# Multiplying the repeated u by B for two groups in one VectorE instruction

## The chip, the cores and the metric

The kernel runs on one core of a Trainium2 chip. The metric is the device time of one execution in microseconds. The kernel before took 5985.74 us (median of 3 runs, 5984.24 to 5988.39).

## What is computed

The input x is (4, 128, 64, 64) in float32. Layer 0 is a four-head attention over the 4096 positions of each image with a residual and a layer norm. Layer 1, which the change touches, is the sum of a 3x3 convolution, a spectral filter (a 1x1 mix between an rfft2 and an irfft2) and a Mamba block over the 4096 positions. The part that counts here is the selective scan of the Mamba block, for 256 channels with 16 states each:

```python
def step(h, inp):
    xt, dtt, Bt, Ct = inp
    dA = jnp.exp(dtt[..., None] * A)
    h = dA * h + dtt[..., None] * Bt[:, None, :] * xt[..., None]
    y = jnp.einsum('bdn,bn->bd', h, Ct)
    return (h, y)
```

The product dt * x is called u in the kernel. For each channel it is needed 16 times, once per state, each time multiplied by another row of B.

## The kernel before

Layer 0 runs first and writes its result to memory; layer 1 (`layer1`, from L685) starts when it has ended. The 4 images of 4096 positions are cut into 32 items of 512 positions (`NIT`), and the 256 channels x 16 states of an item into G = 32 groups of 128 rows (8 channels x 16 states). Below, g is the number of a group within its item.

Each engine has its own program, written out in order: for each item a loop over g, in which `emit` issues the work on this item and `prepare(it + 1, ...)` a slice of the preparation of the next one. Engines wait for each other with semaphores alone. For one group the work is this:

- TensorE, `repeat_u` (L1021): a 0/1 matmul copies u of 8 channels to 128 rows, in PSUM bank g % 4 (`NU = 4`). It waits until the scan of group g - 4, which read that bank, has ended (L1020).
- VectorE, `times_b` (L1181): multiplies that bank in place by `b_rep`, the rows of B. It waits for the matmul (semaphore `u_rep`).
- ScalarE, `decay` (L1119): exp(dt * A) in `d_a`, on data that SyncE's DMA queue has brought (L885).
- VectorE, the scan (L1195), which writes `hh`; then ScalarE keeps its last column (L1112).
- GpSimd, L1232: multiplies `hh` by C into `hc`.
- TensorE, `sum_states` (L1004): every four groups, it sums 16 states to one channel. It is issued in the slots g = 8, 12, ..., 28, and for the last eight groups in slots 0 and 4 of the next item. The one of slot g reads `hc` of groups g - 8 to g - 5.

VectorE multiplies one group ahead: multiply 0, multiply 1, scan 0, multiply 2, scan 1, and so on. After the scans of g = 5 and g = 21 it adds the skip term (`add_skip`, L1166), which reads the bank that `sum_states` of slots 8 and 24 begins anew (L1002 makes it wait). After the scan of g = 16 it adds one row to the output (L1172), and after the scans of g = 23 and 24 it makes the low part of the next item's u (`low`, L1154).

TensorE works strictly in the order of its program. Between the `repeat_u` of g and of g + 1 stands the other work of slot g, one or two steps in most slots: `sum_states`, a matmul of `prepare`, convolution matmuls by the table `FILLS`. Slot 29 is the longest, with 8 small matmuls in fp32 (L973, L974), and slot 30 has 4 more (L994). After the scan of g = 18 GpSimd also computes dt (L1220), after 19 ux (L1223), and after 22 `gate` (L1215).

The two lines of TensorE that the wait for a bank rests on:

```python
ge(pe, scanned, it * G + g - NU + 1)
nc.tensor.matmul(ps[:, U_BANK + g % NU, :], sel_g[:, j, :], s_u[:, p, s, :], start=True, stop=True).then_inc(u_rep, 1)
```

Of the kernel before, what the change touches and what calls it, by code (L numbers as in the profile page):

```python
# [8 lines left out]
ALU = mybir.AluOpType  # L9
# [667 lines left out]
LC = 512  # L677
# [7 lines left out]
def layer1(nc, z_ext, w, out, nb=B):  # L685
# [16 lines left out]
    with ExitStack() as ctx:  # L702
        def sb(name, shape, dt=F32):
            return ctx.enter_context(nc.sbuf_tensor(name, shape, dt))
# [8 lines left out]
        ps = ctx.enter_context(nc.psum_tensor("ps1", [128, 8, CH], F32))  # L713
        U_BANK, Y_BANK, O_BANK, ITEM_BANK = 0, 4, 5, 6
        NU = 4
# [26 lines left out]
        b_rep = sb("b_rep", [128, 2, LC])  # L742
# [19 lines left out]
        with nc.Block() as block:  # L762
            @block.sync
            def _(sp):
                for dst, src in (
                        (win[:, :], w["win"]), (xs[:, :, :, :].rearrange("p a b c -> p (a b c)")[:, 0:4 * INNER],
                                                w["taps"].rearrange("(o k) e -> o (k e)", o=1).to_broadcast([C, 4 * INNER])),
                        (wxd[:, :, :], w["wxd"]), (wdt[:, :], w["wdt"]), (sel_b[:, :], w["sel_b"]), (sel_c[:, :], w["sel_c"]),
                        (hh[:, 0:2, :].rearrange("p a b -> p (a b)"), w["sel_g"]), (sel_y[:, :, :], w["sel_y"]),
                        (wconv[:, :, :], w["wconv"]), (wspec[:, :, :], w["wspec"]), (hilb[:, :], w["hilb"]),  # L770
                        (hil0[:, :], w["hil0"].to_broadcast([128, W])), (wout[:, :, :], w["wout"]), (cols[:, :], w["cols"]),
                        (a_neg[:, :], w["a_log"])):
                    sp.dma_start(dst, src).then_inc(loaded, 16)
                sp.wait_ge(loaded, NLOAD)
# [49 lines left out]
        G = GROUPS  # L824

        def ge(e, s, value):

            if value > 0:
                e.wait_ge(s, value)  # L829

        def column(g):


            half, jj, i = g // 16, g // 4 % 4, g % 4
            return 2 * half + i // 2, jj + 4 * (i % 2)
# [6 lines left out]
        def steps(prepare, emit, tail):  # L842

            for g in range(G):
                prepare(0, 0, g)
            for it in range(NIT):
                emit(it, it % 2)
            tail()

        with nc.Block() as block:  # L850
# [297 lines left out]
            @block.vector  # L1148
            def _(dve):
                def low(j, p, stack, src, part):  # L1150

                    a, b = slice(64 * part, 64 * part + 64), slice(64 - 64 * part, 128 - 64 * part)
                    dve.wait_ge(hi_ready, j * 2 + part + 1)
                    nc.vector.tensor_tensor(stack[b, p, part::2, :], src[a, :, :], stack[a, p, part::2, :].bitcast(F32), ALU.subtract  # L1154
                                            ).then_inc(lo_ready, 1)

                def prepare(j, p, g):
                    if g in (23, 24):
                        low(j, p, s_u, ux, g - 23)

                def add_skip(it, p, half):

                    dve.wait_ge(y_done, it * 8 + 4 * half + 4)

                    ge(dve, o_ready, it)
                    nc.vector.scalar_tensor_tensor(yt[:, half, :], xs[:, p, half, :], cols[:, 4 + half:5 + half], ps[:, Y_BANK, :],  # L1166
                                                   ALU.mult, ALU.add).then_inc(y_added, 1)

                def add_row(it, p):

                    dve.wait_ge(o_copied, it + 1)
                    nc.vector.tensor_tensor(o_sb[:, p, 0:W], o_sb[:, p, 0:W], row0[:, it % STEPS, :], ALU.add).then_inc(o_full, 1)  # L1172

                def times_b(it, p, g):

                    dve.wait_ge(u_rep, it * G + g + 1)
                    if g == 0:
                        dve.wait_ge(item_read, it * NITEM + BI + 1)

                    bu = ps[:, U_BANK + g % NU, :]  # L1180
                    nc.vector.tensor_tensor(bu, bu, b_rep[:, p, :], ALU.mult).then_inc(bu_ready, 1)  # L1181

                def emit(it, p):
                    times_b(it, p, 0)
                    for g in range(G):

                        if g + 1 < G:
                            times_b(it, p, g + 1)
                        s, j = column(g)
                        dve.wait_ge(bu_ready, it * G + g + 1)  # L1190
                        dve.wait_ge(da_ready, it * G + g + 1)

                        ge(dve, hc_ready, it * G + g - NHH + 1)
                        ge(dve, kept, it * G + g - NHH + 1)
                        nc.vector.tensor_tensor_scan(hh[:, g % NHH, :], d_a[:, g % NDA, :], ps[:, U_BANK + g % NU, :],  # L1195
                                                     carry[:, it % STEPS, s * 8 + j:s * 8 + j + 1], ALU.mult, ALU.add).then_inc(scanned, 1)
                        prepare(it + 1, 1 - p, g)
                        if g == 21:
                            add_skip(it, p, 0)
                        if it:  # L1200
                            if g == 5:
                                add_skip(it - 1, 1 - p, 1)
                            if g == 16:
                                add_row(it - 1, 1 - p)

                def tail():
                    add_skip(NIT - 1, 1, 1)
                    add_row(NIT - 1, 1)
                steps(prepare, emit, tail)

            @block.gpsimd
# [108 lines left out]
```

## Time and profile before

| | |
|---|---|
| median of 3 runs | 5985.74 us |
| the profiled execution | 5988.07 us |
| its span | 5986.3 us |
| TensorE busy | 5515.8 us, 92% |
| VectorE busy | 4841.2 us, 81% |
| GpSimd busy | 4207.8 us, 70% |
| ScalarE busy | 3701.3 us, 62% |
| mean granted TensorE clock | 0.982 |

The span is the time between the first and the last instruction of the profiled execution. The shares of the page are means over both layers: layer 1 takes the last 1980 us, about a third. VectorE is busy for 90% or more of every slice of the page from about 4040 us on, and for 70% of most slices of layer 0. In a timeline row the first number is the start and the second the duration in us; VectorE's instructions overlap a little, the next one starting some 0.1 us before the recorded end of the last. So what an instruction costs its engine is the distance from its start to the next start, not its duration.

### The profile page before, as it was taken

The page shows a single profiled execution, that of the slowest core. Times are in us where ns is not written, and L with a number is a line of the kernel's source. Part 1 is how long each engine was busy: PE and PEld are TensorE (multiplying, and loading weights), DVE is VectorE, ACT ScalarE, POOL GpSimd, SP SyncE. Part 2 cuts the span into 40 slices and gives each one's busy share as a digit, 9 for nine tenths or more (in the row PEclk, how much of TensorE's full clock was granted, in tenths as well). Part 3 has the DMA queues.
Part 4 walks back from the last instruction along what each step waited for, and adds up shares of the span by engine and source line. Part 5 has one row for each costly group of instructions (what it writes and reads, how often), then busy time and mean ns, then how long its engine had stood idle before and what let it go on. Part 6 is the DMA issues. An engine that isn't in the chain of part 4 may idle for free. (4 is left out here: it accounts for less than half of the span.)

```text
span 5986.3 us, 84041 instructions
## 1 busy us (share of the span) xinstructions
PE 5515.8 (92%) x27184; PEld 2520.1 (42%) x27184; DVE 4841.2 (81%) x7122; ACT 3701.3 (62%) x7290; POOL 4207.8 (70%) x3213
## 2 busy tenths in 40 slices
PE   7999999999999999999999999968888878888887
PEld 4444444444444444444444444423333333333333
DVE  7777777777777777777777777639999999999999
ACT  3666666665666666666666666656666666666665
POOL 2767666677676677776667776638787887878787
PEclk8999999999999999999999999989999999999999
DMA  4011010110110101101010000024444444454444
GB/s 135 21 43 41 20 38 22 43 40 27 43 35 21 45 20 43 41 24 36 24 26 22 8 22 13 20 94 172 168 161 168 160 169 162 168 168 160 168 160 153
DMA packets 292503, 464.74 MB, mean 78 GB/s; under 512 B 72384, under 2 KB 95808, under 8 KB 290624
## 3 DMA queue, kind: packets, MB, share of 16 engines
q1 hardware_dynamic: 292064, 459.37, 23.6%
q8 instruction: 217, 3.56, 0.2%
q14 instruction: 222, 1.82, 0.1%
HBM read 381.41 MB, written 76.28 MB: 76 GB/s over the span
## 5 line engine op out<-in xcount | busy, mean ns | idle before, releaser
L560 POOL TENSOR_TENSOR sums<-exps 128x512 f32<-128x512 f32 x2048 | 2617.2, 1298 | 1313.2 <-ACT exps L493 1308.3
L569 DVE TENSOR_REDUCE mpart<-ps 128x1 f32<-128x512 f32 x4096 | 2541.6, 683 | 818.9 <-PE ps L369 818.9
L493 ACT ACTIVATE exps<-ps 128x512 f32<-128x512 f32 x4096 | 2127.9, 603 | 1404.0 <-PE ps L376 1403.6
L369 PE MATMUL ps<-k_st,q_ring 96*128 96x512 f32 x4096 | 1753.9, 429 | 17.3 <-DMA k_st<-qk_split 8.9
L1232 POOL TENSOR_TENSOR hc<-hh,c_rep 128x512 f32<-128x512 f32 x1024 | 1361.8, 1338 | 392.3 <-DVE hh L1195 391.9
L376 PE MATMUL ps<-q_ring,k_st 98*128 98x512 f32 x4096 | 1621.7, 397 | 4.0 <-ACT exps L493 3.6
L1195 DVE TENSOR_TENSOR_SCAN hh<-d_a,carry,ps 128x512 f32<-128x512 f32 x1024 | 1308.6, 1281 | 1.0
L369 PEld LDWEIGHTS ps<-k_st,q_ring 96*128 96x128 f32 x4096 | 775.1, 189 | 1063.4 <-DVE mpart L569 508.2
L387 PE MATMUL ps<-exps,v_ring 128*32 128x512 f32 x8192 | 1090.8, 605 | 0.0
L376 PEld LDWEIGHTS ps<-q_ring,k_st 98*128 98x128 f32 x4096 | 777.7, 190 | 148.4 <-ACT exps L493 17.3
L1021 PE MATMUL ps<-s_u,sel_g 128*128 128x512 f32 x1024 | 559.1, 549 | 199.0 <-DVE hh L1195 197.4
L1119 ACT ACTIVATE d_a<-d_a,a_neg 128x512 f32<-128x512 f32 x1024 | 730.8, 720 | 3.6 <-DMA d_a<-dt_dram 2.0
L1181 DVE TENSOR_TENSOR ps<-ps,b_rep 128x512 f32<-128x512 f32 x1024 | 700.8, 687 | 12.6 <-PE ps L1021 11.6
L1021 PEld LDWEIGHTS ps<-s_u,sel_g 128*128 128x128 f32 x1024 | 194.7, 191 | 870.0 <-DVE hh L1195 752.8
L399 PE MATMUL ps<-sums,ones_d 128*32 128x512 f32 x4096 | 533.1, 592 | 0.0
L1004 PE MATMUL ps<-hc,sel_y 128*32 128x512 f32 x2048 | 287.2, 633 | 183.6 <-DVE yt L1166 114.7
L387 PEld LDWEIGHTS ps<-exps,v_ring 128*32 128x32 f32 x8192 | 161.2, 108 | 416.9 <-ACT exps L493 361.2
L1112 ACT COPY carry<-hh 128x1 f32<-128x1 f32 x1024 | 186.7, 183 | 238.8 <-DVE hh L1195 238.5
L939 PE MATMUL ps<-za,wtap 128*128 128x512 f32 x528 | 266.0, 598 | 27.2 <-DMA stage_j<-z_ext 27.2
L986 PE MATMUL ps<-zp,wconv 128*128 128x512 f32 x576 | 290.0, 604 | 0.0
L399 PEld LDWEIGHTS ps<-sums,ones_d 128*32 128x32 f32 x4096 | 133.0, 110 | 306.6 <-issue 298.1
L1064 ACT CAST s_u<-ux 64x1024 fp32r<-64x1024 f32 x66 | 68.9, 1045 | 286.0 <-POOL ux L1223 285.2
(106 smaller groups left out, 3075.4 us busy)
## 6 DMA issues: line engine op xcount, KB each, us to landing
d_a<-dt_dram SPq DMA_DIRECT2D x1040, 256.0 KB
qk_split<-hilo SPq DMA_DIRECT2D x128, 256.0 KB, 2.3
q_ring<-qk_split SPq DMA_DIRECT2D x384, 64.0 KB, 2.0
k_st<-qk_split SPq DMA_DIRECT2D x45, 512.0 KB, 7.1
dt_dram<-dt SPq DMA_DIRECT2D x33, 512.0 KB, 2.8
za<-z_ext SPq DMA_DIRECT2D x33, 320.0 KB, 3.8
zp<-z_ext SPq DMA_DIRECT2D x32, 320.0 KB, 6.6
xc<-in_x SPq DMA_DIRECT2D x32, 256.0 KB, 3.0
```

The source lines that it names most:

```text
L369: nc.tensor.matmul(d_bank(("max", m, t)), q_ring[0:PARTS, m % 4, 128 * i:128 * i + 128], k_st[0:PARTS, g % 2, chunk(kc)], start=True, stop ...
L376: nc.tensor.matmul(a_bank(("exp", n, t)), k_st[0:SHIFT, n // NCH % 2, 128 * t:128 * t + 128], q_ring[0:SHIFT, n % 4, :], start=True, stop= ...
L387: ins = nc.tensor.matmul(ps[D * i:D * i + D, OUT_BANK, :], v_ring[:, n // NCH % 2, 4 * v + i, :], exps[:, (2 * v + i // 2) % 4, CH * (i % ...
L399: nc.tensor.matmul(ps[D * j:D * j + D, DEN_BANK, :], ones_d[:, :], sums[:, u % 8, :], start=(v == 1), stop=(v == QUADS - 1)).then_inc(sum_ ...
L493: nc.scalar.activation(exps[:, u % 4, CH * half:CH * half + CH], a_bank(("exp", n, t)), ACT.Exp, scale=SCALE).then_inc(a_done, 1)
L560: pool.tensor_tensor(sums[:, u % 8, :], exps[:, u % 4, 0:CH], exps[:, u % 4, CH:2 * CH], ALU.add).then_inc(summed, 1)
L569: nc.vector.tensor_reduce(mpart[:, m % 2, t % 4, t // 4:t // 4 + 1], d_bank(("max", m, t)), AX.X, ALU.max).then_inc(d_done, 1)
L1021: nc.tensor.matmul(ps[:, U_BANK + g % NU, :], sel_g[:, j, :], s_u[:, p, s, :], start=True, stop=True).then_inc(u_rep, 1)
L1119: nc.scalar.activation(d_a[:, g % NDA, :], d_a[:, g % NDA, :], ACT.Exp, scale=a_neg[:, s * 8 + j:s * 8 + j + 1]).then_inc(da_ready, 1)
L1181: nc.vector.tensor_tensor(bu, bu, b_rep[:, p, :], ALU.mult).then_inc(bu_ready, 1)
L1195: nc.vector.tensor_tensor_scan(hh[:, g % NHH, :], d_a[:, g % NDA, :], ps[:, U_BANK + g % NU, :], carry[:, it % STEPS, s * 8 + j:s * 8 + j ...
L1232: pool.tensor_tensor(hc[:, g % NHC, :], hh[:, g % NHH, :], c_rep[:, p, :], ALU.mult).then_inc(hc_ready, 1)
```

## The change

The multiplication takes two groups at a time: groups 2k and 2k + 1 lie in neighbouring banks, and one instruction of 1024 columns multiplies both by B, which is read twice by a broadcast of its 512 columns. It waits for the `repeat_u` of both. Pair 0 is multiplied ahead of scan 0, and pair k + 1 is issued ahead of the scan of the odd group 2k + 1. Every scan waits for the multiplication of its pair. The number of banks, and TensorE's program with its waits, are as before.

```diff
-                def times_b(it, p, g):
-
-                    dve.wait_ge(u_rep, it * G + g + 1)
-                    if g == 0:
+                def times_b(it, p, k):
+
+                    dve.wait_ge(u_rep, it * G + 2 * k + 2)
+                    if k == 0:
                         dve.wait_ge(item_read, it * NITEM + BI + 1)
 
-                    bu = ps[:, U_BANK + g % NU, :]
-                    nc.vector.tensor_tensor(bu, bu, b_rep[:, p, :], ALU.mult).then_inc(bu_ready, 1)
+                    bu = ps[:, U_BANK + 2 * k % NU:U_BANK + 2 * k % NU + 2, :]
+                    b = b_rep[:, p, :].rearrange("p (o l) -> p o l", o=1).to_broadcast([128, 2, LC])
+                    nc.vector.tensor_tensor(bu, bu, b, ALU.mult).then_inc(bu_ready, 1)
 
                 def emit(it, p):
                     times_b(it, p, 0)
                     for g in range(G):
 
-                        if g + 1 < G:
-                            times_b(it, p, g + 1)
+                        if g % 2 and g + 1 < G:
+                            times_b(it, p, g // 2 + 1)
                         s, j = column(g)
-                        dve.wait_ge(bu_ready, it * G + g + 1)
+                        dve.wait_ge(bu_ready, it * (G // 2) + g // 2 + 1)
                         dve.wait_ge(da_ready, it * G + g + 1)
```

The order of VectorE before, from the skip addition of g = 21 to the multiplication of g = 28 (the instruction on L1195 is the scan):

```order
L1166 SCALAR_TENSOR_TENSOR yt<-xs,cols,ps 128x512 [waits o_ready,y_done]
L1181 TENSOR_TENSOR ps<-ps,b_rep 128x512 [waits u_rep]
L1195 SCALAR_TENSOR_TENSOR hh<-d_a,carry,ps 128x512 [waits hc_ready,kept,da_ready,bu_ready]
L1181 TENSOR_TENSOR ps<-ps,b_rep 128x512 [waits u_rep]
L1195 SCALAR_TENSOR_TENSOR hh<-d_a,carry,ps 128x512 [waits hc_ready,kept,da_ready,bu_ready]
L1154 TENSOR_TENSOR s_u<-ux,s_u 64x2x512 [waits hi_ready]
L1181 TENSOR_TENSOR ps<-ps,b_rep 128x512 [waits u_rep]
L1195 SCALAR_TENSOR_TENSOR hh<-d_a,carry,ps 128x512 [waits hc_ready,kept,da_ready,bu_ready]
L1154 TENSOR_TENSOR s_u<-ux,s_u 64x2x512 [waits hi_ready]
L1181 TENSOR_TENSOR ps<-ps,b_rep 128x512 [waits u_rep]
L1195 SCALAR_TENSOR_TENSOR hh<-d_a,carry,ps 128x512 [waits hc_ready,kept,da_ready,bu_ready]
L1181 TENSOR_TENSOR ps<-ps,b_rep 128x512 [waits u_rep]
```

And the order after the change, from the same addition to the first scan of the next item (L1182 is the multiplication, L1196 the scan; x3 stands for the scans of g = 29, 30 and 31):

```order
L1166 SCALAR_TENSOR_TENSOR yt<-xs,cols,ps 128x512 [waits o_ready,y_done]
L1196 SCALAR_TENSOR_TENSOR hh<-d_a,carry,ps 128x512 [waits hc_ready,kept,da_ready,bu_ready]
L1182 TENSOR_TENSOR ps<-ps,b_rep 128x1024 [waits u_rep]
L1196 SCALAR_TENSOR_TENSOR hh<-d_a,carry,ps 128x512 [waits hc_ready,kept,da_ready,bu_ready]
L1154 TENSOR_TENSOR s_u<-ux,s_u 64x2x512 [waits hi_ready]
L1196 SCALAR_TENSOR_TENSOR hh<-d_a,carry,ps 128x512 [waits hc_ready,kept,da_ready,bu_ready]
L1154 TENSOR_TENSOR s_u<-ux,s_u 64x2x512 [waits hi_ready]
L1182 TENSOR_TENSOR ps<-ps,b_rep 128x1024 [waits u_rep]
L1196 SCALAR_TENSOR_TENSOR hh<-d_a,carry,ps 128x512 [waits hc_ready,kept,da_ready,bu_ready] x2
L1182 TENSOR_TENSOR ps<-ps,b_rep 128x1024 [waits u_rep]
L1196 SCALAR_TENSOR_TENSOR hh<-d_a,carry,ps 128x512 [waits hc_ready,kept,da_ready,bu_ready] x3
```

Each multiplication of two groups now stands one scan, not two, behind the scan that frees its second bank: the multiplication of groups 24 and 25 follows the scan of 22, and bank 25 % 4 is freed by the scan of 21. Before, the multiplication of 25 followed the scan of 23.

## Rows read from the trace of the kernel before

**Rows 1.** Busy us in one stretch: PE, PEld, DVE, ACT, POOL; then PE clock, DMA

```profile
4800.00:5200.00 400.00, 325.33 (x1143) 130.88 (x1144) 397.58 (x450) 266.89 (x569) 319.90 (x235) 0.96 0.49 166
```

**Rows 2.** Groups by line, 4400 to 5900 us: busy us, mean ns, idle before

```profile
L1195 DVE TENSOR_TENSOR_SCAN hh<-d_a,carry,ps 128x512 f32<-128x512 f32 x781 | 998.0, 1280 | 0.8
...
L1181 DVE TENSOR_TENSOR ps<-ps,b_rep 128x512 f32<-128x512 f32 x780 | 533.8, 687 | 6.3 <-PE ps L1021 5.5
```

**Rows 3.** Waits of VectorE, 4150 to 5950 us: total us, times, longest

```profile
DVE ps L1181 <- PE ps L1021: 6.4, 15, 0.5
```

**Rows 4.** Timeline of VectorE, g = 14 to 23: start, duration, instruction

```profile
5015.61 1.28 DVE L1195 TENSOR_TENSOR_SCAN hh<-d_a,carry,ps 128x512 f32<-128x512 f32 x1
5016.80 0.69 DVE L1181 TENSOR_TENSOR ps<-ps,b_rep 128x512 f32<-128x512 f32 x1
...
5022.82 1.29 DVE L1195 TENSOR_TENSOR_SCAN hh<-d_a,carry,ps 128x512 f32<-128x512 f32 x1
...
5029.31 0.74 DVE L1166 SCALAR_TENSOR_TENSOR yt<-xs,cols,ps 128x512 f32<-128x512 f32 x1
5029.95 0.72 DVE L1181 TENSOR_TENSOR ps<-ps,b_rep 128x512 f32<-128x512 f32 x1
```

**Rows 5.** Timeline of VectorE, same item, g = 23 to the next item's g = 0

```profile
5033.65 1.22 DVE L1154 TENSOR_TENSOR s_u<-ux,s_u 64x1024 fp32r<-64x1024 f32 x1
5034.79 0.68 DVE L1181 TENSOR_TENSOR ps<-ps,b_rep 128x512 f32<-128x512 f32 x1
5035.51 1.28 DVE L1195 TENSOR_TENSOR_SCAN hh<-d_a,carry,ps 128x512 f32<-128x512 f32 x1
5036.82 1.50 DVE L1154 TENSOR_TENSOR s_u<-ux,s_u 64x1024 fp32r<-64x1024 f32 x1
5038.34 0.70 DVE L1181 TENSOR_TENSOR ps<-ps,b_rep 128x512 f32<-128x512 f32 x1
...
5045.86 0.70 DVE L1181 TENSOR_TENSOR ps<-ps,b_rep 128x512 f32<-128x512 f32 x1 [0.33 <-PE ps L1021]
...
5048.24 2.44 DVE L1195 TENSOR_TENSOR_SCAN hh<-d_a,carry,ps 128x512 f32<-128x512 f32 x2
5050.60 1.27 DVE L1181 TENSOR_TENSOR ps<-ps,b_rep 128x512 f32<-128x512 f32 x2
5051.78 1.27 DVE L1195 TENSOR_TENSOR_SCAN hh<-d_a,carry,ps 128x512 f32<-128x512 f32 x1
```

**Rows 6.** Timeline of TensorE, same item: slots 18, 24, 25, 28 to 31

```profile
5016.95 0.50 PE L1021 MATMUL ps<-s_u,sel_g 128*128 128x512 f32 x1 [0.41 <-DVE hh L1195]
...
5030.20 1.07 PE L1004 MATMUL ps<-hc,sel_y 128*32 128x512 f32 x8 [1.81 <-DVE yt L1166]
5031.20 0.50 PE L1021 MATMUL ps<-s_u,sel_g 128*128 128x512 f32 x1
...
5039.49 1.94 PE L1004 MATMUL ps<-hc,sel_y 128*32 128x512 f32 x8 [2.15 <-POOL hc L1232]
5041.36 0.80 PE L1021 MATMUL ps<-s_u,sel_g 128*128 128x512 f32 x1
...
5045.22 0.61 PE L1021 MATMUL ps<-s_u,sel_g 128*128 128x512 f32 x1
...
5046.48 0.71 PE L1021 MATMUL ps<-s_u,sel_g 128*128 128x512 f32 x2
```

**Rows 7.** Timeline of GpSimd, same item: hc of g = 22, gate, hc of g = 23

```profile
5033.74 2.26 POOL L1232 TENSOR_TENSOR hc<-hh,c_rep 128x512 f32<-128x512 f32 x1
...
5035.97 1.26 POOL L1215 TENSOR_TENSOR yt<-yt,gz 128x512 f32<-128x512 f32 x1
5037.20 2.24 POOL L1232 TENSOR_TENSOR hc<-hh,c_rep 128x512 f32<-128x512 f32 x1
```

**Rows 8.** Line L794, once at the start of layer 1: duration ns

```profile
L794 DVE TENSOR_TENSOR wtap<-xs,win x1: 1220/1220/1220, 3967.6 to 3967.6; 128x1024 f32<-128x1024 f32 x1
```

**Rows 9.** Timeline of VectorE in layer 0: L588 waits for L586

```profile
3032.56 0.27 DVE L586 CAST mrow<-ps 4x128 fp32r<-4x128 f32 x1
3032.86 0.28 DVE L588 TENSOR_TENSOR mrow<-ps,mrow 4x128 fp32r<-4x128 f32 x1
```

## The prediction, made before the changed kernel ran

> **What bounds the kernel now.** I read the table of stretches first. In layer 1 VectorE is busy for 397.58 of 400 us, TensorE for 325, GpSimd for 320, ScalarE for 267 [rows 1]: VectorE is the bound, and whatever it is spared is gained, whatever it waits is lost. The groups by line say what fills it: scans of 1280 ns and multiplications of 687 ns, with next to no idle time ahead of them [rows 2]. The waits say the same: VectorE waited for the repeated u for 6.4 us in 1800 [rows 3]. So the question is not only what the pairing spares VectorE, but whether that wait stays so small.
>
> The timeline gives the true costs, start to next start. Scan to multiplication: 5015.61 to 5016.80, 1.19 us [rows 4]. Two multiplications in a row and then a scan: 5050.60 to 5051.78, so 0.59 each; two scans in a row take 2.44, of which the last is about 1.26 recorded, so scan to scan is 1.18 [rows 5]. The skip addition costs 0.64 (5029.31 to 5029.95) [rows 4].
>
> **What it removes and adds.** Two multiplications (2 x 0.59 = 1.18 us) become one of 1024 columns, 512 times (16 in each of 32 items). No row has that one on PSUM. A VectorE multiplication of 1024 columns with a broadcast operand in SBUF records 1220 ns [rows 8], 533 more than the 687 of 512 columns [rows 2]; the low part, also 1024 columns, records 1.22 and lets the next start after 1.14 [rows 5]. The floor is 0.59 + 0.53 = 1.12. I take 1.13, a gain of 0.05 a pair, 0.8 us an item, 26 us in all. The dear end is the second low part, 1.52 from start to start [rows 5], which would be a loss of 0.34 a pair; that row holds a collision explained below, so I don't take it.
>
> The Trainium skill ("VectorE: DVE Perf Modes", The TRN2 errata) gives a float32 tensor_tensor (N + 151)/0.96 ns and says that a fixed cost is paid per instruction. The recorded 687 and 1220 agree with it. By that rule a merge would spare 0.157 us a pair, 80 us in all; the starts in rows 4 and 5 show that two thirds of this fixed part already lies under the neighbour, so the sum takes 0.05.
>
> **What it moves.** TensorE's program and waits stay, VectorE's order changes. The repeat of u for 2k + 1 may begin when the scan of 2k - 3 has ended, since it takes that scan's bank. Before, its multiplication stood two scans and two multiplications later: over 3 us of slack. Now the multiplication of pair k stands right behind one scan, that of 2k - 2. Count from the start of scan 2k - 3: it ends at 1.28, TensorE starts 0.06 later (5016.89 to 5016.95), the matmul takes 0.50 [rows 4, 6], and VectorE goes on 0.03 behind it (5045.22 + 0.61 to 5045.86) [rows 5, 6]. That is 1.87; the multiplication is wanted at 1.19 + 1.19 = 2.38. So 0.51 us of slack are left. An even slot may still hold up to 2 us of other TensorE work ahead of the repeat of the odd group; the fullest ones hold a sum, 1.00 us (5030.20 to 5031.20 [rows 6]), and one fp32 matmul of about the same, and just fit. Going through the slots of FILLS and `prepare` pair by pair, I find the repeat in time except in three places.
>
> *Pairs 4 and 12.* Slots 8 and 24 hold a sum that waits for the skip addition, and the repeat of 9 and 25 is queued behind it. From the start of the addition (5029.31): the sum starts at 0.89, the repeat at 1.89 (5031.20), ends at 2.39, VectorE goes on at 2.42 [rows 4, 6]. Wanted: 0.64 for the addition, 1.19 for a scan, 1.83. Stall 0.59, twice an item.
>
> *Pair 15, the largest.* The repeat of 31 is queued behind the sum of slot 28, the repeat of 29, the 8 matmuls of slot 29, the repeat of 30 and slot 30. From the start of that sum to the start of the repeat of 31 it takes 5046.48 - 5039.49 = 6.99 us, and 0.50 to its end [rows 6]. The sum itself waits for GpSimd's hc of group 23 (2.15 us here), and GpSimd is working off a backlog that began at g = 18. Before, the multiplication of 31 was wanted last of all and never late; only that of 30 waited, 0.33 [rows 5]. Now it is wanted ahead of scan 29.
>
> The second half of an item, from the start of scan 18 (5022.82 [rows 4]) as zero. Before, the first scan of the next item starts at 5051.78, 28.96 [rows 5]. After, in VectorE's order: multiplication 10 at 1.19, scans 19 and 20 at 2.32 and 3.50, pair 11 at 4.69, scan 21 at 5.82, addition 7.01, scan 22 at 7.65, pair 12 at 7.01 + 2.42 = 9.43, scan 23 at 10.56, low part 11.88 (scan to low part is 1.31, [rows 5]), scan 24 about 13.1 to 13.3, second low part 14.4 to 14.6.
>
> Here it meets GpSimd. The hc of 22 took 2.26 us and that of 23 took 2.24, where the gate took 1.26 [rows 7]: each had a low part beside it, which started at 5033.65 and 5036.82 [rows 5]. The second low part started while the gate ran to 5037.23 and took 1.50 instead of 1.22. So whichever of the two starts second waits for the other. The Trainium skill ("GPSIMD Engine Reference", the table of its specifications) says that GpSimd shares its SBUF interfaces with VectorE instructions that have two SBUF inputs; the low part has two, the multiplication by B only one, and these rows agree.
>
> In the new order the second low part comes 0.4 to 0.6 us later than before (14.0 there). Either it still goes first; hc 23 then ends 0.4 later, the sum of slot 28 starts at 16.67 + 0.4 = 17.1, and the repeat of 31 has ended at 17.1 + 7.5 = 24.6. Or hc 23 goes first and the low part waits a microsecond: then pair 13 is at 16.8, scan 25 ends at 19.2, the repeat of 29 starts at 19.3, and by the same rows (5041.36 to 5046.48 is 5.12, and 0.50) that of 31 ends at 24.9, less a little. Both give pair 15 at about 24.7; its own order would want it at 22.9 to 23.8. Stall 1 to 1.8 us.
>
> From 24.7: multiplication 1.13, three scans 3.55, then the multiplication of pair 0 of the next item. Its scan 0 must wait for it directly, where before a second multiplication lay between: 1.22 to its recorded end and 0.03 for the wait, as in layer 0 (5032.83 to 5032.86) [rows 8, 9], 1.25 for 1.18. Scan 0 starts at 30.63, against 28.96: **+1.67 us**.
>
> *First half*, scan 0 to scan 18: nine pairs spare 9 x 0.05 = 0.45; the stall of pair 4 costs 0.59. The row addition after scan 16 also has two SBUF inputs, and the hc of 15 now still runs when it starts, as two scans stand in a row: some 0.2. **+0.34 us.** In the second half the gains of pairs 10 to 14 are swallowed, since pair 15 waits for TensorE anyway.
>
> Sum: 2.0 us an item, 32 items, +64 us. On the profiled execution's 5988.07 that is 6052, on the median of 5985.74 (2.3 below it) **6050 us**.
>
> **The rivals.**
>
> *Faster.* VectorE alone decides, and TensorE is always in time: 512 x 0.05 = 26 us less, 5960 (with 0.157 a pair, the page's figure, 5906). For it: a wait of only 6.4 us now and TensorE at 81%. Against it: the repeat of 31 ends 7.5 us behind a sum that GpSimd dates, and that is no mean but a fixed point of each item. It decides if that repeat ends before 22.9 in the count above.
>
> *Only the small stalls.* The stall of pair 15 doesn't appear, because hc 23 comes early (a full microsecond earlier, if it escapes the low part) and scan 25 isn't held. Per item: 15 pairs and the boundary spare 0.68, the two stalls of 0.59 and the row addition cost 1.38; +0.7, 22 us, 6008.
>
> *The slack of 0.51 is too small everywhere.* A repeat of u at the low clock records 0.80 for 0.50 (5041.36 [rows 6]); with longer even slots on top each pair would wait about 0.3. That adds 9 x 0.3 in the first half, 86 us more: 6136. It decides if TensorE's granted clock, 0.96 now [rows 1], falls in the idle times that the new order makes.
>
> *The instruction across two banks is dear.* At 1.52 it costs 0.39 more than I take, 11 times an item where it counts: +137 us, 6187. For it there is no row, against it the broadcast row of 1220 ns, which is in SBUF.
>
> *The change does what it says*, by the order of instructions; that it has no effect would need gain and stalls to cancel, near 5986.
>
> **Chances and range.** Forecast 0.64, faster 0.07, only the small stalls 0.12, slack too small 0.07, dear instruction 0.04, cancelling 0.06. About 0.2% (12 us) is what a measurement of this kernel can tell from no change. Faster by more than that 0.07, within it 0.06, slower 0.87. My own case spans 6028 (the sum of slot 28 no later than before, no cost at the row addition) to 6066 (both low parts late); the range for 8 in 10 reaches to the small stalls and a little above: 6003 to 6076.
>
> **What would show it.** The profile after should have: 512 multiplications recorded at about 1220 ns; waits of that line for TensorE of some 3 us an item, near 100 us in all instead of 6.4, in three places (g = 8, 24 and 30) and hardly elsewhere; the repeat of 31 still about 7 us behind the sum of slot 28; hc 23 at about 2.2 us, or the second low part at over 2. An item should take 2 us more. The prediction is wrong if waits sit at most pairs, if the multiplication is far from 1220 ns, or if the last pair of an item doesn't wait.

## The result, and the profile after

The changed kernel took 6054.65 us (median of 4 runs, 6048.09 to 6061.99) against 5986.19 us before: a ratio of 1.0114, 95% interval 1.010 to 1.0129, so 68 us slower; 6050 had been forecast. Every ratio is against runs of the kernel before on the same chip. On another chip the changed kernel took 6063.94 us (ratio 1.0127, 1.0113 to 1.0141).

The page of the profiled execution (6061.99 us, the longest of its four runs), its first lines and the multiplication's row:

```profile
span 6060.2 us, 83529 instructions
PE 5497.7 (91%) x27184; PEld 2550.1 (42%) x27184; DVE 4852.7 (80%) x6610; ACT 3706.3 (61%) x7290; POOL 4195.9 (69%) x3213
L1182 DVE TENSOR_TENSOR ps<-ps,b_rep 128x1024 f32<-128x1024 f32 x512 | 621.0, 1213 | 75.9 <-PE ps L1021 74.9
```

The busy time of all VectorE work went up by 11.5 us, though 512 instructions are gone. Of it, the multiplications went from 700.8 us (1024 of 687 ns) to 621.0 (512 of 1213 ns). The idle time ahead of them was 12.6 us on the page of before, and is 75.9.

The stretch that answers to [rows 1], 4800 to 5200 us:

```profile
4800.00:5200.00 400.00, 308.15 (x1102) 132.36 (x1101) 383.83 (x333) 253.56 (x536) 309.18 (x227) 0.95 0.46 156
```

The groups by line that answer to [rows 2] (4400 to 5900 us), and the waits that answer to [rows 3] (4150 to 5950 us):

```profile
L1182 DVE TENSOR_TENSOR ps<-ps,b_rep 128x1024 f32<-128x1024 f32 x377 | 457.2, 1213 | 52.6 <-PE ps L1021 51.9
L1154 DVE TENSOR_TENSOR s_u<-ux,s_u 64x1024 fp32r<-64x1024 f32 x46 | 82.9, 1802 | 1.4
...
L1172 DVE TENSOR_TENSOR o_sb<-o_sb,row 128x64 f32<-128x64 f32 x24 | 8.4, 349 | 0.0
```

```profile
DVE ps L1182 <- PE ps L1021: 60.4, 84, 2.0
```

VectorE was busy for 397.58 of 400 us before, now for 383.83. It waits for the repeat of u three times an item (84 waits in 1800 us). The low part (L1154), whose mean in the same view of before was 1359 ns, now records 1802, and the row addition (L1172) 349, which was 217.

VectorE's timeline from scan 20 to the first scan of the next item (start, duration; it answers to [rows 4, 5]). Scan g is the scan of group g, and pair k the multiplication of groups 2k and 2k + 1:

```profile
4999.31 1.25 DVE L1196 TENSOR_TENSOR_SCAN hh<-d_a,carry,ps 128x512 f32<-128x512 f32 x1
5000.49 1.20 DVE L1182 TENSOR_TENSOR ps<-ps,b_rep 128x1024 f32<-128x1024 f32 x1
5001.60 1.26 DVE L1196 TENSOR_TENSOR_SCAN hh<-d_a,carry,ps 128x512 f32<-128x512 f32 x1
5002.79 0.71 DVE L1166 SCALAR_TENSOR_TENSOR yt<-xs,cols,ps 128x512 f32<-128x512 f32 x1
5003.43 1.27 DVE L1196 TENSOR_TENSOR_SCAN hh<-d_a,carry,ps 128x512 f32<-128x512 f32 x1
5005.19 1.23 DVE L1182 TENSOR_TENSOR ps<-ps,b_rep 128x1024 f32<-128x1024 f32 x1 [0.49 <-PE ps L1021]
5006.33 1.27 DVE L1196 TENSOR_TENSOR_SCAN hh<-d_a,carry,ps 128x512 f32<-128x512 f32 x1
5007.63 1.52 DVE L1154 TENSOR_TENSOR s_u<-ux,s_u 64x1024 fp32r<-64x1024 f32 x1
5009.18 1.28 DVE L1196 TENSOR_TENSOR_SCAN hh<-d_a,carry,ps 128x512 f32<-128x512 f32 x1
5010.49 2.09 DVE L1154 TENSOR_TENSOR s_u<-ux,s_u 64x1024 fp32r<-64x1024 f32 x1
5012.61 1.23 DVE L1182 TENSOR_TENSOR ps<-ps,b_rep 128x1024 f32<-128x1024 f32 x1
...
5020.17 1.23 DVE L1182 TENSOR_TENSOR ps<-ps,b_rep 128x1024 f32<-128x1024 f32 x1 [0.50 <-PE ps L1021]
5021.31 3.61 DVE L1196 TENSOR_TENSOR_SCAN hh<-d_a,carry,ps 128x512 f32<-128x512 f32 x3
5024.85 1.21 DVE L1182 TENSOR_TENSOR ps<-ps,b_rep 128x1024 f32<-128x1024 f32 x1
5026.09 1.28 DVE L1196 TENSOR_TENSOR_SCAN hh<-d_a,carry,ps 128x512 f32<-128x512 f32 x1
```

Read the distances of the starts. Pair 11 costs 1.11 (5000.49 to 5001.60) where two multiplications cost 1.18. Pair 12 stands 1.76 behind its scan (5003.43 to 5005.19) where 1.19 is the rule: a stall of 0.57, of which the row shows 0.49 as idle. The low parts cost 1.55 and 2.12 from start to start, 1.14 and 1.52 before. Scan 0 follows pair 0 after 1.24.

TensorE in the same item, from the repeat of 29 to that of 31 (it answers to the last rows of [rows 6]; x2 in the last row holds the repeat of 31 and the next one), and the granted clock there (PEclk, the third column from the end):

```profile
5015.08 0.79 PE L1021 MATMUL ps<-s_u,sel_g 128*128 128x512 f32 x1 [2.46 <-DVE hh L1196]
...
5018.53 0.48 PE L1021 MATMUL ps<-s_u,sel_g 128*128 128x512 f32 x1
...
5019.66 0.71 PE L1021 MATMUL ps<-s_u,sel_g 128*128 128x512 f32 x2
```

```profile
5015.00:5020.00 5.00, 4.92 (x28) 4.76 (x28) 4.67 (x5) 2.26 (x7) 3.93 (x4) 0.69 0.53 204
```

TensorE idled 2.46 us until scan 25 ended and then worked at a granted clock of 0.69 on average, that is partly at its low level, 1.2 GHz. How long the low level lasts differs from item to item. In the item above the repeats of 29 and 31 lie 4.6 us apart and pair 15 waits 0.50. In the item 135 us later the low level lasts longer:

```profile
5142.10 0.80 PE L1021 MATMUL ps<-s_u,sel_g 128*128 128x512 f32 x1 [2.46 <-DVE hh L1196]
...
5147.96 0.72 PE L1021 MATMUL ps<-s_u,sel_g 128*128 128x512 f32 x2
```

The distance is 5.9 us, and pair 15 waits 1.79. Over the 32 items of the trace the distance is 4.6 to 6.0 us and the wait of pair 15 0.50 to 2.02, 1.19 on average. The waits of pairs 4 and 12 are 0.5 to 0.65 each in every item (but for pair 4 of the very first).

The kernel before had the low clock here too, but in half of its items only. In the 16 items in which the repeat of 29 records 0.80, as in [rows 6], the repeats of 29 and 31 start 5.1 to 5.25 us apart; in the other 16, as in the item behind that of [rows 6], 3.3:

```profile
5101.09 1.07 PE L1004 MATMUL ps<-hc,sel_y 128*32 128x512 f32 x8 [1.12 <-POOL hc L1232]
5102.08 0.50 PE L1021 MATMUL ps<-s_u,sel_g 128*128 128x512 f32 x1
...
5105.41 0.51 PE L1021 MATMUL ps<-s_u,sel_g 128*128 128x512 f32 x1
```

GpSimd beside it (it answers to [rows 7]):

```profile
5004.32 3.75 POOL L1233 TENSOR_TENSOR hc<-hh,c_rep 128x512 f32<-128x512 f32 x3
5008.02 2.26 POOL L1216 TENSOR_TENSOR yt<-yt,gz 128x512 f32<-128x512 f32 x1
5010.23 3.48 POOL L1233 TENSOR_TENSOR hc<-hh,c_rep 128x512 f32<-128x512 f32 x2
```

hc g is GpSimd's multiplication by C of group g. The first low part starts at 5007.63 while hc 22 runs to 5008.07, and records 1.52; the gate, which started behind it, is drawn out to 2.26. The second starts at 5010.49, just after hc 23 (5010.23), and waits for that one: 2.09.

An item, from first low part to first low part, took 61.41 us before (mean of 31) and 63.83 after: 2.42 more, 77 us in 32 items, in the profiled execution, whose span is 74 longer.

One regularity of the second half explains several of the experiments. Counted from the start of scan 18, the first low part starts at 11.8 us on average, and scan 24 behind it at 13.33, and this distance is the same, 13.33 to 13.35 on average, in every run below that leaves the low parts and the place of the pairs alone, though in them the first low part starts anywhere from 11.2 to 12.0. It waits for hc 22, so GpSimd's series sets where it ends. What VectorE gains or loses between scan 18 and the first low part is lost or made good there.

### The profile page after: what moved, and what is told of

Read it like the earlier page. It is cut to its first block and busy times, and to the rows that moved or that the text cites. A ratio compares the mean times of both kernels' runs of the same rounds, so it can differ in the third digit from the quotient of the medians.

```text
span 6060.2 us, 83529 instructions
## 1 busy us (share of the span) xinstructions
PE 5497.7 (91%) x27184; PEld 2550.1 (42%) x27184; DVE 4852.7 (80%) x6610; ACT 3706.3 (61%) x7290; POOL 4195.9 (69%) x3213
## 3 DMA queue, kind: packets, MB, share of 16 engines
q14 instruction: 218, 1.79, 0.1%
## 5 line engine op out<-in xcount | busy, mean ns | idle before, releaser
L1233 POOL TENSOR_TENSOR hc<-hh,c_rep 128x512 f32<-128x512 f32 x1024 | 1318.0, 1307 | 479.7 <-DVE hh L1196 462.5
L1196 DVE TENSOR_TENSOR_SCAN hh<-d_a,carry,ps 128x512 f32<-128x512 f32 x1024 | 1259.5, 1263 | 2.2
L1182 DVE TENSOR_TENSOR ps<-ps,b_rep 128x1024 f32<-128x1024 f32 x512 | 621.0, 1213 | 75.9 <-PE ps L1021 74.9
L1004 PE MATMUL ps<-hc,sel_y 128*32 128x512 f32 x2048 | 273.6, 605 | 133.2 <-DVE yt L1166 110.6
```

Of the source, the lines that this page charges most:

```text
L1182: nc.vector.tensor_tensor(bu, bu, b, ALU.mult).then_inc(bu_ready, 1)
L1233: pool.tensor_tensor(hc[:, g % NHC, :], hh[:, g % NHH, :], c_rep[:, p, :], ALU.mult).then_inc(hc_ready, 1)
```

## The experiments

The edits on TensorE leave its work as it is and change its place in the program. Where an item's length is given, it is the mean of 31 in the trace, as above.

**The order without the instruction.**

```diff
-                    nc.vector.tensor_tensor(bu, bu, b, ALU.mult).then_inc(bu_ready, 1)
+                    nc.vector.tensor_tensor(bu[:, 0, :], bu[:, 0, :], b_rep[:, p, :], ALU.mult)
+                    nc.vector.tensor_tensor(bu[:, 1, :], bu[:, 1, :], b_rep[:, p, :], ALU.mult).then_inc(bu_ready, 1)
```

> The changed kernel with the pair multiplied by two instructions of 512 columns, one behind the other, that both wait for both repeats of u: the order of the change without its instruction. My theory: the order makes the loss, the instruction of 1024 columns spares 0.06 us a pair, and where an item is not pinned by TensorE (nine pairs in the first half, pair 15 and pair 0) that saving is lost here: 11 x 0.06 x 32 = 21 us more than the changed kernel's 6055, so 6076 (6070 to 6086). Rival: the 1024-column instruction across two banks is itself the costly part; then this is near the kernel before, 5986 to 6010.

Measured: 6098.31 us, ratio 1.0185 (1.017 to 1.0201), an item 64.85 us. It missed the expected band on the slow side. The rival is out: without the 1024-column instruction the kernel is slower still.

```profile
5026.69 1.32 DVE L1154 TENSOR_TENSOR s_u<-ux,s_u 64x1024 fp32r<-64x1024 f32 x1
...
5034.00 0.80 PE L1021 MATMUL ps<-s_u,sel_g 128*128 128x512 f32 x1 [2.52 <-DVE hh L1196]
...
5039.58 0.71 PE L1021 MATMUL ps<-s_u,sel_g 128*128 128x512 f32 x2
```

An item is 1.02 us longer than in the changed kernel. It is tempting to read this as 16 x 0.06, but the trace divides it otherwise. The first half, scan 0 to scan 18, is 0.54 longer, nine pairs of 0.06. In the second half the first low part starts 0.19 later, which costs nothing: it records 1.32 instead of 1.52, and scan 24 stands at 13.33 as before. Pair 13, pair 15 and pair 0 add 0.06 each. The rest, 0.3, is TensorE's: the repeats of 29 and 31 stand 5.6 us apart in every item, for 5.24 on average in the changed kernel; the granted clock from 5034 to 5040 us was 0.57. So the low clock lasted longer than in the mean item of the changed kernel. Why it did isn't shown. So the multiplications alone account for some 0.7 an item, 23 us, close to the 21 that I had put in, and the miss is the clock's.

**Half of slot 29 behind the repeat of 31.**

```diff
-                    elif g == 29:
-                        begin(j, GI)
-                        pe.wait_ge(flipped, j * 2 + 2)
-                        for i in range(LC // 128):
+                    elif g in (29, 31):
+                        if g == 29:
+                            begin(j, GI)
+                            pe.wait_ge(flipped, j * 2 + 2)
+                        for i in ((0, 1) if g == 29 else (2, 3)):
...
-                        ins.then_inc(item, 1)
+                        if g == 31:
+                            ins.then_inc(item, 1)
```

> The changed kernel with half of slot 29's eight small matmuls moved to slot 31, behind the repeats of u of 30 and 31, which then come 1.7 us earlier. My theory: the wait of pair 15 (about 1.1 us an item on average) goes: 6055 - 1.15 x 32 = 6018 (6010 to 6028); waits of VectorE for the repeat about 40 us in all instead of 75. Rival, the slack is too small at every pair or the low parts decide: 6045 or more.

Measured: 6028.95 us, ratio 1.007 (1.0055 to 1.0085), an item 62.72, one microsecond above the expected band. The waits fell to 33.7 us in the stretch where the changed kernel has 60.4; of pair 15's only 0.5 in 12 of 32 items is left. It is 26 us less than the changed kernel's median, 37 expected; against the profiled execution (62.72 for 63.83 an item) it is 36.

**The sum of slot 8 later.**

```diff
                         repeat_u(it, p, g)
+                        if g - 1 in (8,):
+                            sum_states(it, (g - 1) // 4 - 2)
...
-                        if g >= 8 and g % 4 == 0:
+                        if g >= 8 and g % 4 == 0 and g not in (8,):
```

> The changed kernel with the sum of slot 8 issued behind the repeat of u of group 9 instead of ahead of it. My theory: the stall of pair 4 goes, 0.58 us an item, and nothing swallows it: 6055 - 18.6 = 6036 (6031 to 6042). Rival, that stall is hidden or comes back later in the item: 6050 to 6060.

Measured: 6046.09 us, ratio 1.0099 (1.0082 to 1.0115), an item 63.12. The wait of pair 4 is gone from the trace, and the item is 0.71 shorter by the two profiled executions, where 0.58 was expected. By the medians it is only 9 us in all, less than the 13 to 24 expected. The runs of both scatter by 6 to 14 us, and the changed kernel was not run on this chip, so the size stays open, not the direction of the trace.

**All three moves** (slots 8, 24 and 29).

> The changed kernel with both moves and the sum of slot 24 issued behind the repeat of 25. My theory: no wait of VectorE for the repeat of u is left. Against the kernel before an item gains 16 x 0.06 = 1.0 us and loses some 1.0 to the low parts (1.52 and 2.09 us instead of 1.22 and 1.50), 0.15 to the row addition and 0.07 to the direct wait of scan 0: 5985 to 5998, central 5992. Rival, the three TensorE stalls are symptoms and the pairing itself costs: above 6020.

Measured: 6011.97 us, ratio 1.0043 (1.0028 to 1.0058), an item 62.16: 20 above what was expected. The waits in the stretch of [rows 3] are 6.1 us in all, as many as before the change (6.4). The rest is in the low parts:

```profile
5103.99 3.74 POOL L1237 TENSOR_TENSOR hc<-hh,c_rep 128x512 f32<-128x512 f32 x3
...
5106.70 2.11 DVE L1158 TENSOR_TENSOR s_u<-ux,s_u 64x1024 fp32r<-64x1024 f32 x1
5107.69 2.24 POOL L1220 TENSOR_TENSOR yt<-yt,gz 128x512 f32<-128x512 f32 x1
...
5110.15 2.09 DVE L1158 TENSOR_TENSOR s_u<-ux,s_u 64x1024 fp32r<-64x1024 f32 x1
```

With pair 12 in time the first low part comes 0.6 earlier against GpSimd's series (3.74 us, to 5107.73), and waits 0.6 longer for it: 2.11 instead of 1.51. What the move of slot 24 gained, the collision took.

**The low parts later**, in the changed kernel.

```diff
-                    if g in (23, 24):
-                        low(j, p, s_u, ux, g - 23)
+                    if g in (27, 28):
+                        low(j, p, s_u, ux, g - 27)
```

> The changed kernel with the two low parts issued behind the scans of 27 and 28 instead of 23 and 24, when GpSimd's backlog is over. My theory: each then costs about 1.15 us from start to start instead of 1.54 and 2.12, and since VectorE reaches scan 25 earlier and has the low parts between it and pair 15, the wait of pair 15 goes too: -1.36 - 1.22 = -2.6 us an item, 6055 - 83 = 5972 (5962 to 5986), the waits of pairs 4 and 12 (0.5 recorded each) staying. Rival: the low parts meet GpSimd in their new place as well and only the wait of pair 15 goes: 6016.

Measured: 5987.45 us against 5987.73 of before, ratio 1.0001 (0.9991 to 1.001), an item 61.43. Both low parts record 1.22, and pair 15 no longer waits: the whole loss of the change is gone. The run doesn't say which of the two weighs more, since the low parts now also stand between scan 25 and pair 15 and give TensorE time. By the distances in the traces they are about equal: from start to start the low parts take 2.50 us instead of 3.66, and the stall of pair 15 was 1.3. It just misses the expected band, since I had taken the saving off the median of 6055 and not off the item of 63.83, and 2.4 came, not 2.6. Now GpSimd is the one that waits, which costs nothing there: its hc that starts 0.05 us behind a low part takes 2.30 us.

```profile
5040.91 1.22 DVE L1154 TENSOR_TENSOR s_u<-ux,s_u 64x1024 fp32r<-64x1024 f32 x1
5040.96 2.30 POOL L1233 TENSOR_TENSOR hc<-hh,c_rep 128x512 f32<-128x512 f32 x1 [0.41 <-DVE hh L1196]
```

**All three moves and the low parts**, with pairs, and as a control the kernel before with the same four moves.

> All three moves of TensorE's work and the low parts behind the scans of 27 and 28. My theory: no wait and no collision is left; 62.16 us an item less 2 x 0.97 for the low parts and 0.21 for the last wait, 60.0 an item: 6012 - 69 = 5943 (5935 to 5958), faster than both kernels. Rival (collisions stay): 5980 to 6010.

> The kernel before, with its multiplications of 512 columns and its order, and the same four moves: the control of the last one. Its low parts cost 1.15 and 1.52, so 0.37 an item goes, and the wait of 0.21 ahead of multiplication 30: 61.41 - 0.58 = 60.83, 5987 - 18 = 5969 (5960 to 5978). The difference to the kernel with pairs is then what pairing is worth when nothing waits: 16 x 0.06 less 0.07 for scan 0 and 0.15 for the row addition, 0.74 an item, 24 us in favour of pairs. Rival (the moves themselves gain, pairing doesn't): this one is as fast as the one with pairs or faster.

Measured: 5985.76 us with pairs (ratio 0.9997, 0.9987 to 1.0006; an item 61.37), 5991.49 without (1.0007, 0.9997 to 1.0016; 61.63). Both missed, by 28 and by 13 us above their bands. The 24 us that pairs were to gain over the control came out as 6, and since each of the two kernels has stalls of its own, that is no clean price of pairing. In the kernel with pairs, new waits stand at pair 1 (0.37 in 28 of 32 items), pair 2 (0.16) and pair 14 (0.46), 30 us in all. TensorE's rows at the start of an item show the first two:

```profile
5101.91 0.50 PE L1023 MATMUL ps<-s_u,sel_g 128*128 128x512 f32 x1 [2.42 <-DVE s_u L1158]
...
5104.94 1.91 PE L939 MATMUL ps<-za,wtap 128*128 128x512 f32 x2
5105.86 1.42 PE L1023 MATMUL ps<-s_u,sel_g 128*128 128x512 f32 x1
```

The repeat of group 0 waits 2.42 us for the low part that now comes late, and behind that idle time a convolution matmul (two records, x2) takes 1.91 for 1.02 and a repeat 1.42; the granted clock from 5102 to 5107 us was 0.62. Without pairs no multiplication waits at all, but the first low part records 2.00 on average: with the multiplications of 512 columns it meets GpSimd at another point, which I haven't followed further.

**Every pair one scan later**, in the changed kernel.

```diff
-                    times_b(it, p, 0)
                     for g in range(G):
 
-                        if g % 2 and g + 1 < G:
-                            times_b(it, p, g // 2 + 1)
+                        if g % 2 == 0:
+                            times_b(it, p, g // 2)
```

> The changed kernel with every pair multiplied one scan later, directly ahead of its own even scan (pair k + 1 behind the scan of 2k + 1): the repeat of the odd group has 1.19 us more slack, but each even scan follows its own multiplication and waits for it. My theory: the waits of pairs 4 and 12 go (-1.16 an item), that of pair 15 falls by 1.19 where it is longer (-0.9 on average), and 15 more scans wait 0.13 (+1.95): 6055 - 4 = 6051 (6035 to 6070). Rival, the direct wait costs nothing since both are on one engine: 5990.

Measured: 6049.45 us, ratio 1.0106 (1.0089 to 1.0122), an item 63.32, as expected; the rival, that the direct wait costs nothing, is out. VectorE never waited for a repeat in the stretch. Each even scan follows its pair after 1.24 to 1.25 instead of 1.12:

```profile
5008.61 1.21 DVE L1182 TENSOR_TENSOR ps<-ps,b_rep 128x1024 f32<-128x1024 f32 x1
5009.85 2.45 DVE L1195 TENSOR_TENSOR_SCAN hh<-d_a,carry,ps 128x512 f32<-128x512 f32 x2
```

With four banks that leaves two usable places for a pair: one scan behind the scan that frees its second bank, with 0.5 us of slack, or directly ahead of its own first scan, which then has to wait for it. Right behind the freeing scan every pair would have to wait: the repeat ends 1.87 us after that scan's start, by the prediction's count, and the pair would be wanted at 1.19.

**Low parts later and the sum of slot 8.**

> Pairs, the low parts behind the scans of 27 and 28, and the sum of slot 8 behind the repeat of 9; slots 24 and 29 as in the changed kernel. With the low parts moved alone an item took 61.43 us, with waits of 0.49 recorded (0.58 lost) at pairs 4 and 12 only. With all three TensorE moves new waits came up at pairs 1, 2 and 14, where TensorE had idled for 2.4 us ahead of the item's first repeat and ran at the low clock. My theory: leaving slots 24 and 29 alone avoids these, and the wait of pair 4 goes by itself: 60.85 an item, 5987 - 18.6 = 5969 (5962 to 5977), faster than both kernels by 0.3%. Rival: the item's length is pinned elsewhere and the wait comes back as another one: 5980 to 5990.

Measured: 5988.28 us, ratio 1.0001 (0.9992 to 1.001), an item 61.45; the rival won. The wait of pair 4 is gone, and in 16 of 32 items one of 1.14 us stands at pair 13, where TensorE worked at a low clock in slot 25 (0.56 granted from 5092 to 5095 us):

```profile
5090.91 1.06 PE L1004 MATMUL ps<-hc,sel_y 128*32 128x512 f32 x8 [1.76 <-DVE yt L1168]
...
5092.24 3.52 PE L986 MATMUL ps<-zp,wconv 128*128 128x512 f32 x4
5094.77 1.27 PE L1021 MATMUL ps<-s_u,sel_g 128*128 128x512 f32 x1
```

The two convolution matmuls of slot 25 (recorded as four) took 3.52 us, for 1.88 in the trace of after. Half of the items times 1.23 (the 1.14 and 0.09 for the lost overlap) is 0.6, all of what pair 4 had given.

**The changed kernel again**, beside the next one.

> The changed kernel once more, beside the others on one chip: its earlier runs lie between 6048 and 6062. My theory: what varies is the wait of pair 15, which depends on where TensorE's clock falls and rises against slot 29; the item's length in the trace goes with the sum of those waits. 6048 to 6062, and the waits for the repeat between 60 and 75 us in all. Rival: the spread is noise of the whole program; then the items outside the waits differ as well.

Measured: 6063.94 us (6062.77 to 6064.83), 2 us above the expected band, an item 63.78; pair 15 waits mostly 0.5, 0.7 and 2.0 in turn, 1.14 on average, and the waits in the stretch of [rows 3] are 60.6 us. Outside the waits the items are those of the first trace, so for the items the rival is out. The profiled execution is 2.6 us longer than the first chip's, though its items are 1.6 shorter in sum: layer 1 begins 4 us later. The four runs on the first chip go with the mean granted clock: 6048.09 us at 0.982, 6051.17 at 0.981, 6058.12 at 0.979, 6061.99 at 0.977, and the four here stand at 0.976 to 0.977. So a large part of the 9 us between the medians is the same spread that the first chip shows within itself, and it goes with the clock. Traces exist of the slow end of it alone, so which waits are shorter in the fast runs isn't shown.

**The sum of slot 24 later**, alone.

> The changed kernel with the sum of slot 24 behind the repeat of 25, alone. My theory: the wait of pair 12 (0.58 lost) goes, and the first low part, which then meets GpSimd earlier in the same hc, waits as much longer (2.1 recorded for 1.5): no gain, 6049 to 6060. Rival: the stalls add up, 6055 - 18.6 = 6036.

Measured: 6070.87 us, ratio 1.014 (1.0124 to 1.0155), 11 above the band, which stood on the first chip's median, and 7 above the changed kernel on the same chip; an item 63.98. The stalls don't add up, so the rival is out. The row of its low parts says where the gain of pair 12 went: 2106 ns on average, for 1802. The 7 us more are in pair 15, which waits 1.36 on average instead of 1.14.

```profile
L1156 DVE TENSOR_TENSOR s_u<-ux,s_u 64x1024 fp32r<-64x1024 f32 x46 | 96.9, 2106 | 1.4
```

**More work for TensorE**, in its idle time ahead of the repeat of 29.

```diff
+                        if g == 28:
+                            begin(it + 1, GI)
+                            for n in range(2):
+                                nc.tensor.matmul(bank(GI), wmix[:, 2, :], za[:, 1 - p, W:W + LC], start=True, stop=True)
```

> The changed kernel with two extra fp32 matmuls of 512 columns at the end of slot 28, into the bank that slot 29 overwrites; their result isn't used. They stand where TensorE idles for 2.46 us ahead of the repeat of 29, and would take about 1.7 us of it. In the trace slots 29 and 30 run at the low clock behind that idle time: the repeats of 29 and 31 start 4.6 to 5.9 us apart. My theory: with TensorE kept busy slot 29 runs at the high clock, the repeat of 31 comes some 2 us earlier and the wait of pair 15 goes, though TensorE has more to do: 6055 to 6064 before, less 1.15 to 1.25 x 32 = 6015 to 6027. Rival: the low clock there has another cause, or the extra work delays the repeat of 29: 6050 to 6075.

Measured: 6023.06 us (6019.12 to 6025.81), ratio 1.0057 (1.0043 to 1.007), an item 62.48. TensorE's rows and the granted clock of the stretch:

```profile
5057.77 1.98 PE L1043 MATMUL ps<-za,wmix 128*128 128x512 f32 x4
5060.30 0.51 PE L1021 MATMUL ps<-s_u,sel_g 128*128 128x512 f32 x1 [0.54 <-DVE hh L1200]
...
5062.34 0.48 PE L1021 MATMUL ps<-s_u,sel_g 128*128 128x512 f32 x1
...
5063.77 0.50 PE L1021 MATMUL ps<-s_u,sel_g 128*128 128x512 f32 x1
```

```profile
5060.00:5065.00 5.00, 3.92 (x27) 3.32 (x27) 5.00 (x6) 3.68 (x10) 3.72 (x3) 1.00 0.52 203
```

The added matmuls (L1043, each recorded twice) fill the idle time, 0.54 of 2.46 us is left, the clock is at its high level, and the repeats of 29 and 31 lie 3.5 us apart instead of 4.6 to 6.0. Pair 15 doesn't wait in any item, the waits of pairs 4 and 12 and the low parts are as they were, and an item is 1.36 us shorter. So the kernel with more work is 30 to 40 us faster, and the wait of pair 15 is the low clock's.

## Why the prediction was right

*What bounds the kernel*, VectorE in layer 1: right. What VectorE waits or is held, an item takes longer.

*The pair's cost*, 1.13 us with 1.12 as the floor: 1.11 to 1.14 measured (1.14 behind a wait). The gain is 0.06 a pair, as the first half of the items without the instruction shows from the other side (0.54 for nine pairs). An estimate worked out from the Trainium skill's (N + 151)/0.96 ns ("VectorE: DVE Perf Modes", The TRN2 errata) is 0.157 a pair. It holds for the recorded durations here (2 x 687 - 1213 = 161 ns) and not for the starts; the measurement decides.

*Pairs 4 and 12*: 0.59 forecast, 0.57 measured (0.49 of it recorded), in just these places. But the stall of pair 12 costs nothing by itself: without it the first low part waits as much longer, as the move of slot 24 alone showed. The slack that the old order had was 2.9 us by the prediction's own numbers (4.73 to the multiplication, less 1.87), not over 3; nothing hangs on it.

*Pair 15*: a stall of 1 to 1.8 forecast, 0.6 to 2.1 measured, 1.3 on average. The path was right in its second form, and to the tenth: from scan 18, scan 25 was to end at 19.2 and the repeat of 29 to start at 19.3, and it starts at 19.24; the repeat of 31 was to end at 24.9 and ends at 24.97. But the size has luck in it. I took 5.1 us between the repeats of 29 and 31 from one item of before and called it the length of the slots. It was the length at the low clock, and half of the items of before have 3.3. Read from one of those, the same count would have had the repeat of 31 end at 23.1 and pair 15 in time, at the 23.74 where it stands when it doesn't wait; the sum would have been some 1 us an item lower, near 6020. That the low clock would come in every item after the change was reasoned nowhere. It came with the 2.46 us for which TensorE now waits for scan 25, and with that gap filled the stall is gone. For the same reason the repeat of 31 stands 8.1 us and more behind the sum of slot 28, not the 7 given as a sign, and VectorE's waits sum to 75 us, not to near 100.

*The meeting with GpSimd*: I left open which goes first. It was GpSimd: the second low part takes 2.09. In sum the two low parts lose 1.0 us against before. With pair 15 hanging on scan 25 they and its stall add up, and moving the low parts away took both, 67 us.

*Scan 0 and the row addition*: 1.24 for a forecast of 1.25, and 0.27 instead of 0.12 from start to start, for a forecast of 0.2 more.

*The sum*: the first half of an item was forecast at +0.34 and came to +0.25, from 32.63 to 32.88 us. The second was forecast at +1.67 and came to +2.15, from 28.79 to 30.94 (means of 30 items). Of the 0.5 missing, 0.3 is scan 0, which starts at 30.94 for 30.63, and 0.2 lies in the item the rows came from, which is that much longer than the mean. Together 2.4 in the profiled execution, the longest of its runs; by the medians 2.1, for a forecast of 2.0. That the savings of pairs 10 to 14 are swallowed was right for all but pair 13, though for the first three of them it is the first low part that swallows them.

The rivals are out by the trace: the waits sit in three places and not at every pair, the instruction isn't dear, and pair 15 waits. As for the gain of 26 us that the pairing alone would give, no run shows it whole: the kernels with pairs and with the low parts moved are at 61.4 us an item, like the kernel before, since the 0.96 gained goes into waits of about as much. No version here beats the kernel before by more than the measurement can tell; 5985.76 and 5987.73 are the same.

Open stays whether a better place exists for all of them at once, and what makes TensorE's low clock last shorter in one item than in the next.

## What to carry to other kernels

Merging two instructions that use a ring of buffers shortens the slack of the ring, here from 2.9 us to 0.5: count from the release of the second buffer to the merged instruction, with what is queued ahead of the producer, before counting the 0.06 us that the merge spares. Price it by start distances, not by durations. Read a stretch of the producer in several items before taking its length: here it was 3.3 us in one item and 5.2 in the next, by the granted clock. And where three engines are near their bounds, taking one wait away mostly moves it: check the trace for the next one, be it a collision between two engines or a clock that fell in the new idle time.

## What the runs showed of the hardware

- A VectorE instruction with two SBUF inputs and a GpSimd instruction of 1.27 us exclude each other for nearly their whole length: whichever starts second is drawn out, VectorE's from 1.22 to 2.11, GpSimd's to 2.24 to 2.33. The multiplications and scans, with one input in PSUM, never showed it: in the trace of after none records more than 1.23 and 1.28 us.
- TensorE's idle time costs twice: behind an idle time of 2.46 us it worked at a mean granted clock of 0.69 in one item, and the stretch that takes 3.5 us at the high level took 4.6 to 6.0; two matmuls without use put into that gap made the kernel 30 to 40 us faster.
- A VectorE instruction of 1024 columns across two PSUM banks, read and written in place with a broadcast SBUF operand, records 1213 ns, as little as one in SBUF (1220 [rows 8]).
- A VectorE instruction that waits for the one right before it starts 1.24 us behind its start instead of 1.11 to 1.12: 0.13 us more, the recorded end plus 0.03.
